# Output projections at a group's end moved two slots later, the first tile's value product one slot later, and the output weights' splits moved with them

## The reference

```python
q = (x @ Wq.T).reshape(b, s, H, HD).transpose(0, 2, 1, 3)     # H = 32 heads of HD = 128
k = (x @ Wk.T).reshape(b, s, HKV, HD).transpose(0, 2, 1, 3)   # HKV = 8
v = (x @ Wv.T).reshape(b, s, HKV, HD).transpose(0, 2, 1, 3)
q = _rmsnorm(q, q_norm_w)
k = _rmsnorm(k, k_norm_w)
qg = q.reshape(b, HKV, G, s, HD)
scores = jnp.einsum('bkgqd,bksd->bkgqs', qg, k) / math.sqrt(HD)
bias = jnp.where(rel > 0, NEG_INF, slopes[:, :, None, None] * rel)
attn = jax.nn.softmax(scores + bias[None], axis=-1)
out = jnp.einsum('bkgqs,bksd->bkgqd', attn, v)
out = out.reshape(b, H, s, HD).transpose(0, 2, 1, 3).reshape(b, s, H * HD)
return out @ Wo.T
```

## Time and profile before

| | us |
|---|---|
| median of 3 runs | 1619.59 (1617.97 to 1619.84) |
| the profiled execution, its own time | 1617.08 |
| its span, first to last instruction | 1615.3 |
| PE busy | 1511.1 (94% of the span) |
| DVE, ACT, POOL busy | 1115.7, 816.0, 417.9 |
| mean granted PE clock | 0.988 of full speed |

### The profile page before, as it was taken

How to read it: one execution, slowest core, us unless ns; L and a number is a source line. 1 busy time by engine, 2 the same in 40 slices (tenths; PEclk the granted TensorE clock), 3 DMA queues, 4 the chain that set the end, 5 groups by cost and what they waited for, 6 DMA issues and landing times.

```text
span 1615.3 us, 25452 instructions
## 1 busy us (share of the span) xinstructions
PE 1511.1 (94%) x8968; PEld 1172.3 (73%) x8968; DVE 1115.7 (69%) x2866; ACT 816.0 (51%) x2115; POOL 417.9 (26%) x407
## 2 busy tenths in 40 slices
PE   3998999998897899999999999999999999999997
PEld 2863444443786788888888888888888888888776
DVE  5668777770665677677677677677767767767873
ACT  3523555566333455555555555556555555555531
POOL 4102000010543131331322223143133132224333
PEclk9997999999998999999999999999999999999999
DMA  4363443301200010100100000011010010001000
GB/s 149 97 139 54 54 59 49 41 2 56 64 8 24 17 27 1 40 27 1 40 8 19 14 28 27 1 40 27 1 40 27 1 40 7 20 6 35 1 20 33
DMA packets 40207, 54.28 MB, mean 34 GB/s; under 512 B 5776, under 2 KB 21392, under 8 KB 40080
## 3 DMA queue, kind: packets, MB, share of 16 engines
q1 hardware_dynamic: 40080, 52.65, 13.7%
HBM read 44.04 MB, written 8.39 MB: 32 GB/s over the span
## 4 chain that ended last, share of the span: by engine, by line
PE 59%; DVE 5%; issue 5%; ACT 4%; POOL 2%; ACTq 0%; DVEq 0%; POOLq 0%
PE ps L50 17%; PE ps L52 17%; PE ps L51 16%; PE ps L1520 6%; PE ps L1495 2%; DVE ab_qt_l L1772 1%; ACT ab_w_h L1626 1%; ACT ab_squares L1657 1%; DVE ab_pt_l L1780 1%; ACT prob L1645 1%; POOL ab_o_l L1416 1%; PE ps L241 1%; ACT ab_pt_h L1673 0%; PE ps L1497 0%; ACT ab_kt_h L1666 0%
## 5 line engine op out<-in xcount | busy, mean ns | idle before, releaser
L1645 ACT ACTIVATE prob<-prob,ab_neg_max 128x128 f32<-128x128 f32 (+7 forms) x256 | 201.1, 786 | 250.3 <-DVE ab_neg_max L1763 249.2
L1780 DVE TENSOR_TENSOR ab_pt_l<-ps,ab_pt_h 128x512 fp32r<-128x512 f32 x288 | 198.1, 688 | 79.4 <-ACT ab_pt_h L1673 78.5
L1673 ACT CAST ab_pt_h<-ps 128x512 fp32r<-128x512 f32 x288 | 172.1, 598 | 122.3 <-PE ps L1520 121.8
L1763 DVE CUSTOM_DVE_ANT_0 prob<-ps,rel 128x512 f32<-128x512 f32 (+3 forms) x256 | 146.0, 570 | 102.4 <-PE ps L52 101.5
L50 PE MATMUL ps<-ab_w_h,ab_xt_h 128*128 128x512 f32 (+1 forms) x512 | 186.3, 364 | 6.8 <-DVE ab_v_l L1800 6.6
L1041 DVE TENSOR_REDUCE ra_part_max<-ps 128x1 f32<-128x512 f32 (+3 forms) x318 | 156.5, 552 | 47.8 <-PE ps L943 28.7
L1520 PE MATMUL ps<-ident,prob 128*128 128x128 f32 x1152 | 173.4, 273 | 4.6 <-DVE ab_qt_l L1772 3.3
L1788 DVE TENSOR_SCALAR prob<-prob,ab_recip 128x128 f32<-128x128 f32 (+7 forms) x256 | 169.3, 661 | 9.1
L52 PE MATMUL ps<-ab_w_h,ab_xt_l 128*128 128x512 f32 (+1 forms) x512 | 174.1, 340 | 0.0
L51 PE MATMUL ps<-ab_w_l,ab_xt_h 128*128 128x512 f32 (+1 forms) x512 | 173.5, 339 | 0.0
L1405 POOL TENSOR_TENSOR ab_rms<-ab_ms_eps,neg_half 128x5 f32<-128x5 f32 x64 | 76.2, 1191 | 311.5 <-DVE ab_ms_eps L1805 310.6
(11 more groups left out here) (231 smaller groups left out, 3482.6 us busy)
## 6 DMA issues: line engine op xcount, KB each, us to landing
f_raw<-in_wqkv SPq DMA_DIRECT2D x32, 384.0 KB, 3.7
f_raw<-in_wbo SPq DMA_DIRECT2D x32, 256.0 KB, 2.6
ra_first_rows<-parts SPq DMA_DIRECT2D x36, 128.0 KB, 7.1
parts<-pa_stage SPq DMA_DIRECT2D x12, 256.0 KB, 2.9
parts<-f_raw SPq DMA_DIRECT2D x12, 256.0 KB, 3.4
ra_q_st<-parts SPq DMA_DIRECT2D x24, 128.0 KB, 6.0
ra_k_st<-parts SPq DMA_DIRECT2D x24, 128.0 KB, 6.6
f_raw<-in_wf SPq DMA_DIRECT2D x8, 324.0 KB, 3.3
```

The lines of the kernel that those rows point to most:

```text
L1645: act.activation(prob[:, t % 2, h, 0:w], prob[:, t % 2, h, 0:w], ACT.Exp, bias=neg_max[:, t % 2, h, pieces_per_head(t % NT) - 1:pieces_per ...
L1673: act.copy(pt_h[:, n % PT, :], ring_bank("p", u, j)).then_inc(pt_high, 1)
L1763: dve.tensor_tensor_reduce(out=prob[:, t % 2, h, k0:k1], in0=ps[:, n % 2, a:b], in1=const["rel"][:, SLIDE - i * P + k0:SLIDE - i * P + k1] ...
L1780: dve.tensor_tensor(pt_l[:, n % PT, :], ring_bank("p", u, j), pt_h[:, n % PT, :].bitcast(F32), ALU.subtract).then_inc(emptied, 1)
```

## The change

`project_out` of the last tile (u % 8 = 7) and of the first tile (u % 8 = 0) of groups 0 to 6 moves from slot 7 of step u + 2 to slot 1 of step u + 3, on PE and with its addition on DVE. In the last group both stay in slot 7. The first tile's `mix` moves from slot 4 to slot 5 and ACT's copy of it from slot 5 to slot 6. The splits of the new output weights move too: on ACT from slot 7 of step 1 and slots 0 and 1 of step 2 to slots 2, 3 and 4 of step 2; on POOL from slots 0 to 3 to slots 4 to 7 of step 2, in all 8 groups.

```diff
 def mixed_in(t, s):
     u, j = (t - 1, s - 4) if s >= 4 else (t - 2, s + B_SLOTS - 4)
-    return (u, j) if 0 <= u < B_STEPS and j <= u % NT else None
+    if u % NT == 0:
+        j -= 1
+    return (u, j) if 0 <= u < B_STEPS and 0 <= j <= u % NT else None
+
+def output_in(t, s):
+    late = t - 3 if s == 1 else t - 2
+    u = late if s in (1, 7) and 0 <= late < B_STEPS else None
+    return u if u is not None and (s == 1) == (u < B_STEPS - NT and u % NT in (0, NT - 1)) else None
...
-            if s == 7 and 0 <= t - 2 < B_STEPS:
-                add(t, "o", t - 2)
+            if output_in(t, s) is not None:
+                add(t, "o", output_in(t, s))
...
-                    if i == 2 and s < KC and 0 <= g < KVB:
-                        split_low(2 * KC * g + KC + s)
+                    if i == 2 and s >= KC and 0 <= g < KVB:
+                        split_low(2 * KC * g + s)
...
-                    if s == 7 and 0 <= t - 2 < B_STEPS:
-                        project_out(t - 2)
+                    if output_in(t, s) is not None:
+                        project_out(output_in(t, s))
...
-                    if i == 1 and s == 7 and 0 <= g < KVB:
+                    if i == 2 and s == 2 and 0 <= g < KVB:
                         if g:
                             act.wait_ge(out_done, NT * g)
                         split_high_of(2 * KC * g + KC)
                         split_high_of(2 * KC * g + KC + 1)
-                    if i == 2 and s < 2 and 0 <= g < KVB:
-                        split_high_of(2 * KC * g + KC + 2 + s)
+                    if i == 2 and 3 <= s <= 4 and 0 <= g < KVB:
+                        split_high_of(2 * KC * g + KC + s - 1)
```

More of the change, by code:

```diff
@@ L1861, in step @@
                     second(*half_of(t, s))
-                    if s == 7 and 0 <= t - 2 < B_STEPS:
-                        u = t - 2
+                    if output_in(t, s) is not None:
+                        u = output_in(t, s)
                         dve.wait_ge(out_done, u + 1)
```

## The result

The changed kernel takes 1678.22 us (median of 4 runs, 1677.54 to 1680.27), and the kernel before, run beside it, 1618.78 us (1617.37 to 1619.84). The ratio is 1.037, with a 95% interval from 1.0352 to 1.0388: 59 us slower. The forecast was 1669 us in a range from 1648 to 1682. The direction came out, and the time lies in the range and 9 us above the forecast.

The account below looks back on a forecast made before the run. PE, busy 94% of the span, was taken as the bound. The terms 13.4 + 19.5 + 2.1 + 5.1 + 9.7 = 49.8 us on 1617.1 gave 1666.9, as median 1669 us; range 1648 to 1682.

Parts of the forecast that it names:

- the band that the prediction called its forecast: Whole kernel: a time of 1657 to 1677 us, given a chance of 47%.
- the clock falls in nearly every gap: Rival for the whole kernel: PE's clock halves behind nearly all new gaps, 21 us, giving 1677 to 1684 us; chance 17%.
- Step 1 to step 2: Passage between groups: PE idles 2.61 us before `project`, waiting for `scaled`; loss 1.92 us a passage, 13.4 in 7.
- Step 2 to step 3: First tile's `project_out` leaves step 2, PE idles before `project` in step 3; loss 3.25 us, 19.5 in 6 groups.
- the upper bound: Step 3's gap: DVE's division ends only after POOL's second split, PE idles 3.0 us; 19.5 us against 13.2 at the lower.
- The first group: Step 3 of the group without a passage before it: `project_out` moves behind an existing wait; 2.81 - 0.69 = 2.1 us loss.
- The last group: `project_out` of its first tile stays in slot 7 of step 2 and waits for POOL's moved splits; 5.1 us.
- The clock: PE resumes at half clock behind some new gaps, 1.5 us each; 9.7 us, bounds 0 to 21.
- The argument against many falls: Against the highest clock rival: before 539.63 other gaps were close by, while the passages stand in dense work.
- The argument that 1.9 us had held the clock: After 1.87 us of idle time on PE in the profile the clock held; four transposes there took 0.66 us.
- The rival on the other side: Both chains ready in time, only the waits go: 6.7 us faster, 1612.9 us; needs `scaled` at 656.74; chance 4%.
- At nothing: Effects priced at no cost: unchanged gap before `mix`, ACT's first two casts in slot 2, DVE's addition in slot 1.

Follow-up runs that it names:

- cover7: The changed kernel, but the last tile's output projection stands in slot 0 of step 2, ahead of `project`; 1647.62 us, ratio 1.0175 to the kernel before.
- filled: The changed kernel plus 9 extra matmuls, result overwritten, ahead of `project` in slot 0 of steps 2 and 3; 1660.1 us, ratio 1.0253 to the kernel before.
- splits_after_scaling: The changed kernel, but POOL's second to fourth weight splits in step 2 wait for `scaled` in groups 1 to 7; 1682.17 us, ratio 1.038 to the kernel before.
- tile0_late: The kernel before, with only the first tile's output projection of groups 0 to 6 moved to slot 1 of the step after; 1633.06 us, ratio 1.0083.

## Why the prediction was right, and which term was mis-sized

The direction and the mechanism were right. The time, 1678.22 us, lies outside the band that the prediction called its forecast (1657 to 1677) and inside that of the rival "the clock falls in nearly every gap" (1677 to 1684), which had a chance of 17%. That rival is what came about; the stated range held because it took in most of that band.

The growth of the profiled span is 60.4 us, and the prediction's sum was 49.8. The starts of the first tile's `mix` in both traces (655.05 and 658.26, 786.68 and 796.36, and on to 1444.76 and 1495.36), and of a score near the end (1488.49 and 1548.98), give it by place: 3.2 us up to the first passage, 6.5 in the first group after it, 40.9 in the next five, 9.9 in the last.

- *Step 1 to step 2.* Predicted 1.92 us a passage, project at 2.61 us of idle time. The first passage, where the clock held, shows 1.95, and the idle time is 2.64. The chain ran as worked out: the exponent moved ahead of ACT's copy, the mean square still ended with POOL's row (660.27 and 660.25), and the scaling began at 661.55, right behind `ab_rms`. `cover7` shows that the place before or behind `project` decides. Shown.
- *Step 2 to step 3.* Predicted 3.25 us, the upper bound, with the division behind POOL's split. Without clock falls a group of `filled` is 136.73 - 131.63 = 5.10 us longer; less 1.95 that leaves 3.15. The choice between the bounds was made on 0.03 us and held, and that was luck: by the terms as written, 668.92 + 0.5 + 1.17, POOL is free at 670.59 and not at 670.55, and the division comes up at 670.58. In the trace POOL was ahead by 0.1, since `ab_rms` came only 0.45 us later than before. With the division first the term would have been 13.2 us by the prediction and not 19.5. That the division waits for POOL is shown by `splits_after_scaling`; that most of the rest is lost cover, by `tile0_late`. The 0.36 us between the gaps of these two runs (1.90 and 1.54) agree in sense with the casts on ACT, which no run moved alone.
- *The first group.* Predicted 2.1 us, measured 3.5: the score after `project_out` stands at 546.58, before at 543.31, and the work ahead of the gap ran 0.23 us earlier. The chain was 0.54 us sooner and not 0.69. The rest is the clock: it stayed low through the two `project` calls (4.0 us against 3.68) and into `project_out`, some 1.2 us more than before.
- *The last group.* Predicted 5.1 us for the splits, of which 0.1 are the restart; the wait is 4.89.
- *The clock: the mis-sized term.* I took falls in "half of the 7 first gaps", "a third of the 6 second ones" and the last, 9.7 us. In the change the clock fell behind 6 of the 7 first gaps and all 6 second ones: 12 x 1.52 = 18.2 us, with the last group's and the first group's share about 21. The price of one, 1.5 us, was right, the count was half of what came. The added 11 us close the sum: 49.8 + 11.2 = 61.0 against 60.4. With what the other terms measured it is 13.7 + 18.9 + 2.3 + 4.9 + 20.9 = 60.7. The windows show one case each:

```profile
662.00:668.00 6.00, 5.25 (x26) 4.43 (x27) 1.64 (x8) 0.71 (x2) 0.00 (x0) 1.00 0.00 0
...
800.00:806.00 6.00, 5.15 (x18) 4.32 (x19) 1.69 (x7) 0.71 (x2) 0.00 (x0) 0.72 0.00 0
817.00:823.00 6.00, 5.09 (x18) 4.30 (x19) 2.34 (x7) 0.82 (x2) 2.16 (x2) 0.72 0.61 197
```

  The argument against many falls, that the passages stand in dense work and those of the first group do not, was wrong: dense work before the gap did not save it. The argument that 1.9 us had held the clock rested on one gap of 1.87 us, and gaps of 1.90 us brought falls in `splits_after_scaling`. `filled` shows that it is the idle time and not the matmuls or the transfers, since these are the same there.
- *The rival on the other side,* that both chains are ready in time, failed where it was said to: `scaled` was 2.6 us late in step 2.
- *At nothing* stood the gap before `mix`, the addition on DVE in slot 1 and ACT's first two casts. The first is still 0.32 or 0.33 us in all 7 passages. The others show no wait of PE beyond those that the kernel before had.

## What to carry to other kernels

A wait at the head of a block of matmuls tells what the block is waiting for, and not what the block hides. Before moving it, ask what stands behind it in the same list and what that will wait for: here 0.96 us were to win, and nearly 3 us of cover to lose. If the block can move behind work that doesn't depend on the hidden chain, and stay ahead of the work that does, both are had: the block placed behind one score, and still ahead of `project`, made this kernel 0.23% faster, and giving the low half to DVE, which was free at that moment, made that 0.38%. And where a gap of about 2 us or more opens on PE, price a fall of the clock with it, as a chance and not as a certainty.

## What the runs showed of the hardware

- Whether the clock falls is not decided by a gap's length alone. In `cover7` six gaps of 2.85 us with the same work around them brought it to half in four, and left it at full in two. In the change gaps of 2.64 and 2.85 us brought it down in 12 of 13, but in `splits_after_scaling` gaps of 2.64 us did so in only four of seven, and gaps of 1.90 us in four of six. Behind 1.54 us it held six times of six. What else decides it was not settled.
- The clock can also fall after PE has come back. In `tile0_late` PE was idle for 4.62 us and resumed at full clock at 542.78; it fell within the next microsecond and a half. The stretches, with the granted clock behind POOL's column:

```profile
542.00:543.00 1.00, 0.22 (x1) 0.22 (x2) 1.00 (x4) 0.00 (x0) 0.00 (x0) 1.00 0.00 0
543.00:544.00 1.00, 1.00 (x5) 0.82 (x5) 0.83 (x4) 0.63 (x2) 0.00 (x0) 0.69 0.00 0
544.00:545.00 1.00, 1.00 (x5) 0.90 (x5) 0.00 (x0) 0.18 (x2) 0.00 (x0) 0.50 0.00 0
```

- A division on DVE (f32, SBUF to SBUF, one tensor operand) that comes up while POOL is in a split ends only behind POOL's instruction. Here it took 1.38 us in place of 0.42 and ended at 677.14, with POOL's first split over at 676.94 (a third of the 3.84 us from 675.66). The mean square beside `ab_o_l` took 0.71 us in place of 0.16. Operations with a PSUM source beside the same splits kept their time: the `ab_nat` product took 0.68 us at 677.06. Not every operation of POOL does it: beside `ab_rms` (5 elements a partition, 1.17 us from 660.35) the division of 660.72 took 0.35 us, as it does alone at 256 columns. The Trainium skill (GPSIMD Engine Reference, Key points) names the contention, and the rows beside the splits agree with it.
